# A two-layer transformer block on one core: both attentions rebuilt on row tiles and column strips, with key blocks brought in by DMA

## The chip, the core and the metric

The kernel runs on one core of one Trainium2 chip, as one program. A core has TensorE (matrix multiply), VectorE, ScalarE, GpSimd and SyncE, which here only issues DMAs. The engines run side by side and meet in semaphores. The metric is the time on the device in microseconds; the kernel before took 1709.56 us (median of three runs, 1708.59 to 1713.04).

## The reference, cut to what matters

`x` is 64 batches of 64 rows of 256 columns, `ctx` is 64 batches of 64 rows of 64 columns. There are four stages, each behind a layer norm and a gate.

```python
x = x + tanh(g_xattn[0]) * L0_xattn(layernorm(x), ctx, ctx)   # 32 heads of 8, 8 key heads
x = x + tanh(g_ffn[0])   * L0_ffn(layernorm(x), ...)          # 64 experts, top 8, and a shared one
x = x + tanh(g_xattn[1]) * L1_xattn(layernorm(x), ctx, ctx, Wc, bc)  # 16 heads of 16, 4 key heads, then @ Wc.T + bc
x = x + tanh(g_ffn[1])   * L1_ffn(layernorm(x), ...)          # two products on 8-bit grids
# an attention: the G = 4 query heads of a group share one key head
scores = einsum('bkgsd,bktd->bkgst', qh, kh) * d ** -0.5
out = einsum('bkgst,bktd->bkgsd', softmax(scores), vh)
```

## The kernel before, in words

The 4096 rows lie in SBUF as 32 tiles of 128 rows, two batches each. The program passes over all tiles once per stage, in this order: first attention, routing, experts (96 groups of four row blocks, fetched by SyncE from a DRAM table `xs`, results stored to `ys`), second attention, and the feed-forward. The second attention also adds the expert results into `x`: GpSimd issues 128 of the 256 indirect DMAs for that between its steps (`gather`, L632). While the first attention runs, SyncE loads the expert weights pair by pair (`pair`, L461 and L464, five DMAs), ScalarE rounds them to 16 bits into `region` (L729, L730), GpSimd takes the remainder (L606, L609), and SyncE also writes zeros into `xs` (`pads`, L479 and L481).

An attention is a software pipeline written out by hand for each engine: `step(t, j)` holds what that engine does in step `t` for tiles `t - 3` to `t + 3`, and `sweep` runs the steps from -3 to `LAST`. A tile needs: layer norm written to `XG` (L918, L919), a transpose to `Q1` (L1422, rounded to 16 bits at L738, remainder at L1028), products with the keys whose only use is the row maximum of each head (`maxima`, L1355, reduced at L982), a second transpose that brings remainder and maxima below the queries (`Q2`, L1435, L741), the scores (`scores`, L1369 and L1370), exponentials (L716), the products with the values (`values`, L1381), a copy, a transpose back (L1405), a division by the row sums and the sum into `x` (L1024). Different heads are kept apart by keys and values that are zero outside a head's own rows (`KD1`, `KD2`, `VD`); VectorE writes the key ones from a resident 16-bit copy of all keys, `KH` and its remainder `KL`, times a mask (`diagonal`, L971), and ScalarE the value ones (L757). Scores are products of 16-bit pairs over the whole array.

SyncE's loop in the first attention waits for GpSimd's remainder of pair `n - 2` before it loads pair `n` into the same buffer:

```python
for n in range(2, NPAIR):
    sp.wait_ge(wlo_done, 2 * (n - 1))
    if n > 2:
        sp.wait_ge(d_w, 80 * (n - 2))
    pair(n, stage[n % 2], d_w)
    pads(n - 2)
```

## Time and profile before

| what | value |
|---|---|
| time, median of three runs | 1709.56 us |
| profiled execution, its span | 1714.7 us (no other time is given for that execution) |
| first attention | to 296 us of the span |
| routing, then scatter and first half of the experts | 296 to 828 us |
| second half of the experts | 828 to 1156 us |
| second attention | 1156 to 1530 us |
| feed-forward | from 1530 us |
| busy share: TensorE, VectorE, ScalarE, GpSimd | 69%, 63%, 46%, 52% |
| DMA queue of SyncE | 234192 packets, 169.99 MB |

The shares are means over stages that are limited by different engines, so the rows further down are taken stage by stage. In the trace a row with SPq is SyncE at work on the issue of a DMA: its duration is what the issue costs SyncE, not how long the transfer takes. The boundaries of the stages are where the first and last instructions of their lines lie.

### The profile page before, as it was taken

To read this page: it belongs to the slowest core of one execution; us is meant where nothing else is said; L and a number is where in the kernel's file an instruction comes from. 1 tells how busy PE (TensorE), PEld (TensorE's weight loads), DVE (VectorE), ACT (ScalarE), POOL (GpSimd) and SP (SyncE) were. 2 spreads that over 40 slices of the span, in tenths; PEclk is the share of its full clock that TensorE was granted. 3 is DMA by queue.
4 is the path that set the end of the run, shared out by engine and by line. 5 is a ranking of instruction groups with operands and counts; after the bars stand their busy time and mean duration, and the time that the engine had idled before them with its cause. 6 is when DMAs were issued, how large, how long until landed. Compare 5 with 4: busy or idle time off the path is not lost.

```text
span 1714.7 us, 32329 instructions
## 1 busy us (share of the span) xinstructions
PE 1178.8 (69%) x9122; PEld 778.6 (45%) x9132; DVE 1084.7 (63%) x2699; ACT 783.1 (46%) x1599; POOL 883.5 (52%) x846
## 2 busy tenths in 40 slices
PE   4999998133333299999678777871676777846775
PEld 2566665112221266666555555650454444532243
DVE  5899996666666466666444454442765555747898
ACT  3566665122222166666445454441343333433574
POOL 2343343266666633333377777715888888516100
PEclk9999999555555599999777887785788888878878
DMA  9555554032323599999899999984344434100011
GB/s 209 161 151 154 148 154 135 15 115 104 111 106 110 154 281 308 310 301 304 206 242 237 252 246 248 247 199 101 53 54 55 55 55 55 28 1 1 13 37 49
DMA packets 283470, 247.09 MB, mean 144 GB/s; under 512 B 117584, under 2 KB 270032, under 8 KB 282960
## 3 DMA queue, kind: packets, MB, share of 16 engines
q1 hardware_dynamic: 234192, 169.99, 38.9%
q0 software_dynamic: 49152, 75.53, 20.8%
q8 instruction: 65, 1.06, 0.3%
q14 instruction: 61, 0.50, 0.1%
HBM read 111.93 MB, written 117.77 MB: 134 GB/s over the span
## 4 chain that ended last, share of the span: by engine, by line
DMA 24%; DVE 20%; PE 18%; POOL 16%; issue 13%; SPq 4%; ACT 3%; DVEq 1%; POOLq 0%; ACTq 0%
DMA xs<-V 13%; POOL x L632 11%; DMA arena<-xs 8%; PE bank L1493 4%; DVE arena L1318 3%; DMA xs<-arena,V 2%; PE bank L1369 2%; POOL rs L575 2%; PE bank L1381 2%; DVE arena L971 2%; PE bank L1355 2%; PE bank L1569 2%; PE bank L1370 2%; SPq L518 2%; DVE arena L1316 2%
## 5 line engine op out<-in xcount | busy, mean ns | idle before, releaser
L632 POOL DMA_INDIRECT x<-ys,idx x256 | 404.1, 1578 | 129.2 <-issue 57.6
L650 POOL DMA_INDIRECT xs<-V x192 | 187.1, 974 | 207.7 <-DMA xs<-V 188.5
L1493 PE MATMUL bank<-arena,region 128*128 128x128 f16 x2496 | 253.2, 245 | 1.6 <-ACT arena L834 0.9
L834 ACT COPY arena<-bank 128x640 f16<-128x640 f16 x192 | 132.3, 689 | 190.2 <-PE bank L1569 188.2
L1569 PE MATMUL bank<-arena 128*128 128x128 f16 x1440 | 145.2, 240 | 105.3 <-DMA arena<-xs 101.5
L1381 PE MATMUL bank<-arena 128*72 128x256 f32 (+1 forms) x768 | 212.0, 417 | 0.1
L1493 PEld LDWEIGHTS bank<-arena,region 128*128 (+1 forms) x2496 | 187.0, 111 | 19.2 <-issue 6.2
L1569 PEld LDWEIGHTS bank<-arena 128*128 128x128 f16 x1440 | 97.0, 107 | 113.3 <-DMA arena<-xs 85.4
L573 POOL TENSOR_TENSOR ve<-mv,epsilon 128x1 f32<-128x1 f32 x96 | 39.5, 412 | 202.0 <-DVE mv L912 180.0
L1381 PEld LDWEIGHTS bank<-arena 128*72 128x72 f32 (+1 forms) x768 | 117.2, 158 | 46.4 <-issue 13.5
L982 DVE TENSOR_REDUCE arena<-bank 128x8 f32<-128x512 f32 x192 | 124.1, 675 | 15.5 <-PE bank L1355 14.3
L1422 PE MATMUL bank<-cst,arena 128*128 128x128 f32 x256 | 50.5, 330 | 116.9 <-DVE arena L919 116.8
L716 ACT ACTIVATE arena<-bank 128x512 f32<-128x512 f32 x192 | 107.2, 593 | 27.2 <-PE bank L1370 24.3
L1598 PE MATMUL bank<-region,arena 128*128 x384 | 114.8, 299 | 6.4 <-DVE arena L1255 1.9
L1225 DVE COPY arena<-bank 128x640 f16<-128x640 f16 x96 | 46.7, 487 | 110.1 <-PE bank L1569 108.7
L1599 PE MATMUL bank<-region,arena 64*128 x384 | 113.5, 296 | 0.0
L1242 DVE TENSOR_TENSOR arena<-bank,arena 64x512 f32<-64x512 f32 x96 | 66.5, 693 | 73.0 <-ACT arena L847 73.0
L1624 PE MATMUL bank<-region 128*128 (+1 forms) x246 | 72.6, 430 | 47.1 <-ACT arena L892 17.8
L738 ACT CAST arena<-bank 128x512 f16<-128x512 f32 x64 | 37.4, 584 | 137.4 <-PE bank L1422 137.4
L919 DVE TENSOR_SCALAR arena<-x,mv,rs 128x256 f32<-128x256 f32 (+1 forms) x96 | 40.4, 421 | 92.6 <-POOL rs L575 92.4
L1369 PE MATMUL bank<-arena 128*128 128x256 f16 x384 | 96.6, 281 | 2.4 <-ACT arena L716 2.2
L1370 PE MATMUL bank<-arena 72*128 72x256 f16 (+1 forms) x384 | 95.8, 278 | 0.0
(204 smaller groups left out, 2557.6 us busy)
## 6 DMA issues: line engine op xcount, KB each, us to landing
ys<-arena SPq DMA_DIRECT2D x96, 512.0 KB
arena<-xs SPq DMA_DIRECT2D x288, 160.0 KB
xs<-idx SPq DMA_DIRECT2D x52, 256.0 KB, 2.4
arena<-in_wpairs SPq DMA_DIRECT2D x32, 256.0 KB, 2.6
arena<-in_wpairs SPq DMA_DIRECT2D x128, 64.0 KB, 2.5
x<-ys,idx POOLq DMA_INDIRECT x256, 6.3
out<-arena SPq DMA_DIRECT2D x16, 256.0 KB, 2.2
xs<-idx SPq DMA_DIRECT2D x52, 64.0 KB, 2.1
```

The lines of the kernel that those rows point to most:

```text
L632: pool.indirect_dma_start(tile_x(t), None, ys[t // HT], bass.IndirectOffsetOnAxis(ap=idx[:, t, k:k + 1], axis=0), compute_op=ALU.add).then ...
L650: pool.indirect_dma_start(xs[t // HT], bass.IndirectOffsetOnAxis(ap=at_row[:, t, n % 8:n % 8 + 1], axis=0), ROW[t % NROW], None).then_inc( ...
L716: act.activation(EX[(u + (0 if nsc == 2 else 2 * j)) % 4], bank[4 + u % 2][:, :], ACT.Exp, scale=d ** -0.5).then_inc(a["ex_ready"], 1)
L834: act.copy(XTP[g % 2][q], tpm[n % 2]).then_inc(R_["xt"], 1)
L982: dve.tensor_reduce(XG[j][:, u * gpu:(u + 1) * gpu, 2 * C:C + w], bank[2 + u % 2][:, :].rearrange("p (g k t) -> p g k t", g=gpu, t=S), AX. ...
L1369: pe.matmul(o, KD1[j][:, b, kc], Q1[j][:, :, b * S:(b + 1) * S], start=True, stop=False)
L1370: mm = pe.matmul(o, KD2[j][0:w, b, kc], Q2[j][0:w, :, b * S:(b + 1) * S], start=False, stop=True)
L1381: mm = pe.matmul(bank[6][0:w, b * 256:(b + 1) * 256], VD[j][:, b, p * w:(p + 1) * w], e[:, (p % 2) * 256:(p % 2 + 1) * 256], start=(p == 0 ...
L1493: mm = pe.matmul(o, lhs(a, w, k), rhs(a, w, k), start=(n == 0), stop=(n == 3 * KT - 1))
L1569: mm = pe.transpose(tpm[n % 2][:, m, :], RAW[g % 2][q][:, m * P:(m + 1) * P], rcv("ident"))
L1598: pe.matmul(o, IH[j][:, q, :], wx, start=True, stop=False)
L1599: mm = pe.matmul(o, IL[j][0:I, q, :], wx[0:I], start=False, stop=True)
```

## The change

Keys stay in float32 and are no longer rounded or masked. A ring of four buffers `KD` holds, for tile `t`, each key head on the partitions that its rows of the array have, and in the columns of its head, with zeros elsewhere. The zeros are written once per attention (VectorE before the first, GpSimd before the second), the rows of -1 that subtract the maximum once per buffer and pair of heads (`own_rows`: 16 DMAs of 2 partitions for the first attention, 8 for the second), and the keys themselves tile by tile by SyncE: one DMA per key head and tile (`keys`: eight DMAs of 8 partitions per tile in the first attention, four of 16 partitions in the second). The bulk loads of the transposed context, `KH`, `KL`, `KM` and the `diagonal` are gone.

TensorE's scores are one float32 product of 32 rows per pair of heads in the first attention (64 rows in the second) in place of two 16-bit ones over 128 and 72 rows; the maxima are products of 64 rows by 64 columns with 256 columns streamed (128 in the second); the values go to strips of 32 (64) output columns. Both transposes are of the full 128 by 128. VectorE writes 16-bit key blocks for the maxima from `KD` (`short_keys`, one or two operations on 256 elements), no longer computes a remainder of the queries, and writes the norm once. The value blocks of the first attention go from ScalarE to one GpSimd operation; GpSimd's remainders of the weights move one step later, and so do the values, the transposes back and all behind them: both sweeps are one step longer.

```diff
@@ sizes, tables
-LAST = (NT, NT + 2)
+LAST = (NT + 1, NT + 3)
+NKD = 4
...
-    KH = sb("KH", [P, B, S], F16)
-    KL = sb("KL", [P, B, S], F16)
+    KD = [sb(f"KD{n}", [P, 2, 2 * S]) for n in range(NKD)]
...
@@ SyncE
+            def own_rows(layer):
+                nk, d = LAYERS[layer]
+                a = CW + RCW + TCW + layer * 2 * S
+                rp = 2 * P // nk
+                for q in range(NKD):
+                    for n in range(nk // 2):
+                        at = slice(n * rp + 2 * d, n * rp + 2 * d + 2)
+                        sp.dma_start(KD[q][at], consts[at, a:a + 2 * S].unsqueeze(1).to_broadcast([2, 2, 2 * S])).then_inc(d_own, 16)
+
+            def keys(t, layer):
+                nk, d = LAYERS[layer]
+                if t >= NKD:
+                    sp.wait_ge(A[layer]["sc_ready"], (t - NKD + 1) * nk // 2)
+                for k in range(nk):
+                    at = k // 2 * (2 * P // nk) + k % 2 * d
+                    sp.dma_start(KD[t % NKD][at:at + d, :, k % 2 * S:(k % 2 + 1) * S],
+                                 ctxT[k * d:(k + 1) * d, 2 * t * S:2 * (t + 1) * S].rearrange("c (b s) -> c b s", b=2)).then_inc(d_kd[t % NKD], 16)
...
             for n in range(2, NPAIR):
+                if n + 2 < NT:
+                    keys(n + 2, 0)
                 sp.wait_ge(wlo_done, 2 * (n - 1))
...
+                if g == NG:
+                    sp.wait_ge(kd_zero, 2 * NKD)
+                    own_rows(1)
+                    for t in range(NKD):
+                        keys(t, 1)
...
+            for t in range(NKD, NT):
+                keys(t, 1)
@@ GpSimd, first attention
+                        pool.tensor_tensor(VD[1 - j].rearrange("p b (n h w) -> p (b n) h w", h=2, w=P // nk)[:, :, :, 0:d],
+                                           V[:, bass.ds((t + 1) * 2, 2), :].rearrange("p b (n h d) -> p (b n) h d", h=2, d=d),
+                                           ones[:, 0:2].unsqueeze(1).unsqueeze(3).to_broadcast([P, 2 * npair, 2, d]), ALU.mult).then_inc(a["vd_ready"], 1)
@@ VectorE
-                        diagonal(t + 2, KD1[j], KH, 0, a["kd_ready"])
-                        diagonal(t + 2, KD2[j], KL, 1, a["kl_ready"])
...
-                        dve.tensor_tensor(Q1[j][C:P], bank[0][C:P, :].rearrange("p (g s) -> p g s", g=G),
-                                          Q1[j][C:P], ALU.subtract).then_inc(a["q_ready"], 1)
...
+                def short_keys(t, q):
+                    if past(t, 2):
+                        dve.wait_ge(a["mx_ready"], (t - 1) * nmx)
+                    dve.wait_ge(d_kd[q], kd_done(t, q, layer))
+                    stand_alone(dve, side_v)
+                    for n in range(nk // 4):
+                        mm = dve.tensor_scalar(K16[q % 2][:, :, n * 2 * S:(n + 1) * 2 * S], KD[q][:, :, :], cv(f"part{layer}")[:, n:n + 1], None, ALU.mult)
+                    mm.then_inc(a["k16_ready"], 1)
@@ TensorE
-                            mm = pe.matmul(bank[2 + u % 2][b * S:(b + 1) * S, g * nk * S:(g + 1) * nk * S],
-                                           Q1[j][:, u * gpu + g, b * S:(b + 1) * S], KD1[j][:, b, 0:nk * S],
+                            for r in range(2):
+                                rows = slice(r * 64, (r + 1) * 64)
+                                last[r] = pe.matmul(bank[2 + r][b * S:(b + 1) * S, g * hk * S:(g + 1) * hk * S],
+                                                    Q1[j][rows, gp * 2 * gpu + g, b * S:(b + 1) * S], K16[j][rows, b, 0:hk * S],
+                                                    start=True, stop=True)
...
-                        pe.matmul(o, KD1[j][:, b, kc], Q1[j][:, :, b * S:(b + 1) * S], start=True, stop=False)
-                        mm = pe.matmul(o, KD2[j][0:w, b, kc], Q2[j][0:w, :, b * S:(b + 1) * S], start=False, stop=True)
+                            rows = slice(n * rp, (n + 1) * rp)
+                            mm = pe.matmul(bank[4 + n][:, b * 256:(b + 1) * 256], KD[q][rows, b, :], Q2[q % 2][rows, :, b * S:(b + 1) * S],
                                            start=True, stop=True)
...
-                        mm = pe.matmul(bank[6][0:w, b * 256:(b + 1) * 256], VD[j][:, b, p * w:(p + 1) * w],
-                                       e[:, (p % 2) * 256:(p % 2 + 1) * 256], start=(p == 0), stop=(p == npair - 1))
+                            mm = pe.matmul(bank[1][n * cg:(n + 1) * cg, b * 256:(b + 1) * 256], VD[j][:, b, n * cg:(n + 1) * cg],
+                                           EX[4 * j + n][:, b * 256:(b + 1) * 256], start=True, stop=True)
```

On SyncE the start of the program reads as follows, before and then after. `gate` is the small load of the gates, `V` the values, `x` the input, `in_wpairs` the weights.

```order
L446 DMA gate<-in_g_xattn 128x2
L446 DMA gate<-in_g_ffn 128x2
L451 DMA region<-in_ctxT 64x512 x2
L456 DMA V<-in_ctx 64x8x64 x2
L461 DMA arena<-in_wpairs 128x512
L464 DMA arena<-in_wpairs 64x256 x4
L461 DMA arena<-in_wpairs 128x512
L464 DMA arena<-in_wpairs 64x256 x4
L451 DMA region<-in_ctxT 64x3584 x2
L469 DMA x<-in_x 128x8x256
L456 DMA V<-in_ctx 64x56x64 x2
L471 DMA x<-in_x 128x20x256
```

```order
L445 DMA gate<-in_g_ffn 128x2
L454 DMA KD<-in_consts 2x2x128 x16
L462 DMA KD<-in_ctxT 8x2x64 x16
L468 DMA V<-in_ctx 64x8x64 x2
L476 DMA arena<-in_wpairs 128x512
L479 DMA arena<-in_wpairs 64x256 x4
L476 DMA arena<-in_wpairs 128x512
L479 DMA arena<-in_wpairs 64x256 x4
L462 DMA KD<-in_ctxT 8x2x64 x16
L485 DMA x<-in_x 128x8x256
L468 DMA V<-in_ctx 64x56x64 x2
L487 DMA x<-in_x 128x20x256
```

Four loads of the transposed context have become 48 small ones. In the loop over the pairs, one round on SyncE was and is:

```order
L461 DMA arena<-in_wpairs 128x512
L464 DMA arena<-in_wpairs 64x256 x4
L479 DMA xs<-idx 128x2x512
L479 DMA xs<-idx 128x2x128
L479 DMA xs<-idx 128x2x512
L479 DMA xs<-idx 128x2x128
```

```order
L462 DMA KD<-in_ctxT 8x2x64 x8
L476 DMA arena<-in_wpairs 128x512
L479 DMA arena<-in_wpairs 64x256 x4
L495 DMA xs<-idx 128x2x512
L495 DMA xs<-idx 128x2x128
L495 DMA xs<-idx 128x2x512
L495 DMA xs<-idx 128x2x128
```

The eight loads of keys stand ahead of the pair; rounds 2 to 29 have them, rounds 30 and 31 do not. In the second half of the experts SyncE had the first of these sequences between two groups and has the second, once:

```order
L518 DMA arena<-xs 128x640
L521 ISA
L521 DMA_TRANSPOSE arena<-xs 128x5x128
L527 DMA ys<-arena 128x4x256
L505 DMA V<-in_ctx 64x8x64 x2
```

```order
L539 ISA
L539 DMA_TRANSPOSE arena<-xs 128x5x128
L545 DMA ys<-arena 128x4x256
L454 DMA KD<-in_consts 2x2x128 x8
L462 DMA KD<-in_ctxT 16x2x64 x16
L523 DMA V<-in_ctx 64x8x64 x2
```

There 24 small loads stand between the store of one group and the fetch of a later one.

## Rows read from the trace of the kernel before

**Rows 1.** Windows by stage: busy us and instructions of each engine, granted clock, DMA.

```profile
core 0: us, PE busy (x) PEld busy (x) DVE busy (x) ACT busy (x) POOL busy (x), PEclk, DMA share, GB/s
39.00:296.00 257.00, 247.75 (x1580) 155.97 (x1580) 226.11 (x418) 161.00 (x336) 99.79 (x118) 0.99 0.53 153
828.00:1156.00 328.00, 256.76 (x2485) 189.62 (x2485) 147.01 (x294) 162.24 (x294) 200.28 (x128) 0.79 1.15 239
1156.00:1475.00 319.00, 199.81 (x1130) 133.65 (x1131) 180.68 (x429) 109.25 (x236) 263.09 (x261) 0.78 0.40 60
```

**Rows 2.** Waits of SyncE's queue, 100 to 200 us.

```profile
SPq L461 <- POOL region L609: 35.9, 12, 3.1
```

**Rows 3.** Timeline of SyncE, one row step (start, duration).

```profile
250.20 0.35 SPq L461 DMA_DIRECT2D arena<-in_wpairs  x1
250.60 2.40 SPq L464 DMA_DIRECT2D arena<-in_wpairs  x4
253.04 2.18 SPq L479 DMA_DIRECT2D xs<-idx  x4
258.36 0.35 SPq L461 DMA_DIRECT2D arena<-in_wpairs  x1
```

**Rows 4.** Timeline of SyncE, start of the program.

```profile
2.15 0.51 SPq L446 DMA_DIRECT2D gate<-in_g_xattn  x1
4.43 1.33 SPq L456 DMA_DIRECT2D V<-in_ctx  x2
11.98 1.23 SPq L451 DMA_DIRECT2D region<-in_ctxT  x2
13.88 15.35 SPq L456 DMA_DIRECT2D V<-in_ctx  x2
29.28 5.65 SPq L471 DMA_DIRECT2D x<-in_x  x1
39.02 1.60 SPq L461 DMA_DIRECT2D arena<-in_wpairs  x1
```

**Rows 5.** Issues of three lines: minimum, median, maximum in ns.

```profile
L464 SPq DMA_DIRECT2D arena<-in_wpairs x48: 471/596/599, 103.9 to 195.3; - x48
L451 SPq DMA_DIRECT2D region<-in_ctxT x4: 582/592/596, 3.2 to 12.6; - x4
L518 SPq DMA_DIRECT2D arena<-xs x144: 332/338/2487, 829.5 to 1133.6; - x144
```

**Rows 6.** Groups by line and form, 100 to 260 us.

```profile
L918 DVE TENSOR_SCALAR arena<-x,mv,rs 128x256 f32 x20 | 23.1, 1157 | 1.2
L1028 DVE TENSOR_TENSOR arena<-bank,arena 64x512 f16<-64x512 f32 x20 | 13.9, 695 | 0.6
L971 DVE TENSOR_TENSOR arena<-KL,arena 128x1024 f16<-128x1024 f16 x19 | 13.0, 682 | 0.0
```

**Rows 7.** Timeline of TensorE, 150 to 156 us.

```profile
149.95 0.62 PE L1355 MATMUL bank<-arena 128*64 128x512 f16 x4 [0.16 <-DVE arena L1028]
153.90 1.89 PE L1381 MATMUL bank<-arena 128*72 128x256 f32 x8
155.62 0.60 PE L1435 MATMUL bank<-cst,arena 128*72 128x128 f32 x4
```

**Rows 8.** Timeline of SyncE, second half of the experts.

```profile
841.86 2.34 SPq L518 DMA_DIRECT2D arena<-xs  x3
...
845.66 0.52 SPq L527 DMA_DIRECT2D ys<-arena  x1
846.22 1.87 SPq L505 DMA_DIRECT2D V<-in_ctx  x2
```

**Rows 9.** Groups by line, second attention, 1200 to 1450 us.

```profile
L632 POOL DMA_INDIRECT x<-ys,idx x104 | 166.1, 1598 | 28.7 <-issue 28.7
```

**Rows 10.** Timeline of VectorE, end of the second attention.

```profile
1488.28 0.68 DVE L982 TENSOR_REDUCE arena<-bank 128x8 f32<-128x512 f32 x1
1494.96 0.68 DVE L982 TENSOR_REDUCE arena<-bank 128x8 f32<-128x512 f32 x1
```

More of the change, by code:

```diff
@@ L136, in tile_table, with own_table @@
     return t
-def mask_table():
+def own_table():
     r, out = np.arange(P)[:, None], []
     for nk, d in LAYERS:
-        k = np.arange(nk)[None, :]
-        own = (r % C) // d == k
-        signed = np.where(r < C, r // d == k, -1.0 * (r - C == k))
-        out += [np.repeat(m.astype(np.float16), S, axis=1) for m in (own, signed)]
-    return np.ascontiguousarray(np.concatenate(out, axis=1)).view(np.float32)
+        out.append(np.repeat(-1.0 * (r % (2 * P // nk) - 2 * d == np.arange(2)[None, :]), S, axis=1))
+    return np.concatenate(out, axis=1).astype(np.float32)
 def const_table():
-    return np.concatenate([attention_table(), route_table(), tile_table(), mask_table()], axis=1)
+    return np.concatenate([attention_table(), route_table(), tile_table(), own_table()], axis=1)
 def known(t):
@@ L456, in values @@
                     sp.dma_start(V[half * S:(half + 1) * S, b0:b1, :], ctx[b0:b1].rearrange("b t c -> t b c")).then_inc(d_ctx[part], 16)
-            keys(0)
+            sp.wait_ge(kd_zero, NKD)
+            own_rows(0)
+            for t in range(2):
+                keys(t, 0)
             values(0)
@@ L467, in _ @@
                 pair(n, stage[n], d_stage[n])
-            keys(1)
+            for t in range(2, NKD):
+                keys(t, 0)
             sp.dma_start(x[:, 4:12, :], xv[:, 4:12, :]).then_inc(d_x[1], 16)
@@ L587, in attention @@
                     pool.memset(VD[j].rearrange("p b w -> p (b w)"), 0.0).then_inc(a["vd_set"], 1)
+                for q in range(NKD):
+                    pool.memset(XG[q].rearrange("p g w -> p (g w)"), 0.0).then_inc(a["vd_set"], 1)
                 pool.wait_ge(a["vd_set"], 2)
@@ L619, in attention @@
                             gather(HT, n)
-                        step(t, t % 2)
+                        step(t, t % NKD)
                         if t == -2:
@@ L637, in _ @@
             pool.wait_ge(A[0]["x_done"], NT)
+            for q in range(NKD):
+                pool.memset(KD[q][:, :, :].rearrange("p b t -> p (b t)"), 0.0).then_inc(kd_zero, 1)
             for t in range(0, NT, LNB):
@@ L1386, in step, with maxima @@
-                def step(t, j):
-                    if inside(t + 1):
-                        pe.wait_ge(a["q_ready"], t + 2)
-                        pe.wait_ge(a["kd_ready"], t + 2)
-                        for u in range(nmx // 2):
-                            maxima(t + 1, 1 - j, u)
+                def maxima(t, j, gp):
+                    if past(t, 1) or gp >= 1:
+                        pe.wait_ge(a["mx_done"], t * nmx + 2 * gp)
+                    stand_alone(pe, side_p)
+                    last = [None, None]
+                    for g in range(2 * gpu):
+                        for b in range(2):
+                            for r in range(2):
[3 more added lines that the diff above has]
+                                                    start=True, stop=True)
+                    for mm in last:
+                        mm.then_inc(a["mx_ready"], 1)
@@ new lines, in scores @@
+                def scores(t, q):
+                    if past(t, 1):
+                        pe.wait_ge(a["ex_ready"], t * npair)
+                    rp = P // npair
+                    for b in range(2):
+                        for n in range(npair):
+                            rows = slice(n * rp, (n + 1) * rp)
+                            mm = pe.matmul(bank[4 + n][:, b * 256:(b + 1) * 256], KD[q][rows, b, :], Q2[q % 2][rows, :, b * S:(b + 1) * S],
+                                           start=True, stop=True)
+                            if b:
+                                mm.then_inc(a["sc_ready"], 1)
@@ L1392, in step @@
+                def step(t, q):
+                    j = q % 2
+                    if inside(t - 2):
+                        pe.wait_ge(a["pvs_ready"], t - 1)
+                        for g in range(G):
+                            mm = pe.transpose(bank[1][:, g * P:(g + 1) * P], PVS[:, g, :], ident)
+                        mm.then_inc(a["ot_ready"], 1)
                     if inside(t):
                         pe.wait_ge(a["q2_ready"], t + 1)
-                        pe.wait_ge(a["kl_ready"], t + 1)
@@ L1408, in step @@
-                    if inside(t):
-                        for u in range(nsc, 2 * nsc):
-                            scores(t, j, u)
+                        scores(t, q)
                     if inside(t + 1):
-                        for u in range(nmx // 2, nmx):
-                            maxima(t + 1, 1 - j, u)
+                        for gp in range(1, nmx // 2):
+                            maxima(t + 1, 1 - j, gp)
                     if inside(t + 2):
```

447 lines of the change are left out of this document (201 added, 246 removed).

## The prediction, on record before the changed kernel ran

> **What bounds the kernel now.** I read the stages first. In the first attention [rows 1] the reader should see TensorE busy for 247.75 of 257 us and VectorE for 226.11: both are nearly full, ScalarE and GpSimd are not, and the clock is granted at 0.99. In the second attention GpSimd is busy for 263.09 of 319 us and no other engine comes near. The steps of the first attention repeat every 8.14 to 8.16 us, read from the starts of one SyncE line in two rounds, 250.20 and 258.36 [rows 3].
>
> The engine that the page does not list is the one I looked at longest, since the change gives it most. SyncE works on each DMA that it issues for 0.35 to 0.60 us. One round in the first attention is 0.35 + 2.40 + 2.18 and gaps, from 250.20 to 255.22: 5.02 us for nine DMAs [rows 3]. Then it waits for GpSimd, 35.9 us in 12 rounds, 3.0 us each [rows 2]; from the rows, 258.36 - 255.22 = 3.14 us. That is all the room there is.
>
> **The first attention, compute.** TensorE. Before, a stream of 256 columns in 16 bits takes 256/2.4 = 107 ns if it is alone, one of 512 columns 213 ns, and a float32 product of 256 columns 0.43 us, since four of them (eight instructions) start at 153.90 and the next line at 155.62 [rows 7]. After: 8 scores and 8 values in float32, 16 maxima of 256 columns and 12 transposes at some 0.13 us (the four at 155.62 take 0.60 us with the last one's way out). End to end that is 3.4 + 3.4 + 1.7 + 1.5 = 10.0 us, more than now. Four row tiles or four strips side by side make it 0.9 + 0.9 + 0.4 + 1.5 = 3.7 us. The trace has something of the kind: four maxima of 512 columns in two column halves take 0.62 us in all, where four alone would need 4 x 0.213 = 0.85 [rows 7]. So halves do overlap, and I count on strips and row tiles overlapping too. The Trainium skill says so as well (TensorE: Matmul & The Clock Gate, Part 3: packing small matmuls): matmuls in different row groups or column groups run concurrently, and four row tiles gained 3.07 times there. No run here has shown row tiles yet.
>
> VectorE works 226.11/257 x 8.14 = 7.2 us per step. The remainder of the queries (0.69), both diagonals (0.68 each as listed, which overlap a little, 1.2 together) and the second write of the norm (1157 ns, of which some 0.4 is the operation and the rest waiting beside GpSimd) go [rows 6]; two operations on 256 elements, 0.4 us each, come. That leaves 7.2 - 0.7 - 1.2 - 0.8 + 0.8 = 5.3, up to 6.6 if each of the three tensor-scalar operations waits beside GpSimd as long as the first norm write does now. ScalarE is busy 161.00/257 x 8.14 = 5.1 us and loses the value blocks. The engines that compute could therefore do a step in about 6.5 us.
>
> **The first attention, SyncE.** Each round gets eight more issues, and they must fit into 3.14 us: 0.39 us each. What an issue of 8 partitions and two runs of 64 elements costs no row shows. From below: the fetch of expert rows, 0.338 us at the median [rows 5], some 0.38 with the gap to the next. From above: 1.33 us for two loads of values, 0.67 each [rows 4]. The nearest rows: loads to 64 partitions cost 0.592 to 0.596 us in two different lines, however many bytes they carry [rows 5], and the gates, the smallest load, 0.51 us [rows 4], some 0.55 with the gap. The new loads are narrow and small; I take 0.55 us from start to start. A round is then 5.02 + 8 x 0.55 = 9.4 us, and SyncE no longer waits: TensorE and VectorE wait for it, through the keys (needed two tiles ahead by VectorE) and through the weights (ScalarE copies pair t at the end of its step t). With 0.38 it is 8.1, no step shorter than now; with 0.67 it is 10.4.
>
> Start of the program: 48 such issues instead of four. Up to the gates SyncE needs 2.7 us (one DMA less). From 4.43 to the end of the last load of x at 34.93 there are 30.5 us, less 1.27 for the two context loads at 11.98, so 29.2 us that stay (the long one, 15.35, is a queue that is full, and stays by my estimate) [rows 4]. Round 2 then starts at 2.7 + 29.2 + 48 x 0.55 = 58.3 us, where now it starts at 39.02. 28 rounds with keys at 9.42 us and 2 us for the larger first one end at 324; two without keys, 11 us, at 335; from there the last pair has to land, be split, and the pipeline has to empty, one step more than now, 9 us: 344 us. Now it ends at 296. So +48 us for the stage. The same sum with 0.38: 50 + 230 + 20 = 300, +4 us; with 0.67: 64 + 293 + 20 = 377, +81 us.
>
> The Trainium skill has a sentence that speaks against this whole term (DMA: Bandwidth & Descriptors, Issuing engines are not separate DMA queues): the sequencer's time to initiate a DMA "is usually small relative to the DMA itself". By it the first attention would fall to the step of the compute engines, the rival below. The trace agrees only in part: a weight load takes 0.60 us to issue and 2.4 to land, but the issues are serial and fill 5.02 of 8.14 us.
>
> **The stages behind it.** Routing and scatter wait for the first attention and shift with it, nothing in them is touched; four zero fills on GpSimd lie beside VectorE's statistics: 0. Second half of the experts: SyncE is busy from 841.86 to 848.1 almost without a gap [rows 8], and now issues 24 small loads in one go, 13.2 us at 0.55. The fetches run three groups ahead, about 13 us at the 4.4 us between groups there, but of that the landing of the next fetch has to be paid; the stage also moves data for all its time (DMA share 1.15) [rows 1]. I charge half, +7 us, bounds 0 and +16 (24 x 0.67).
>
> Second attention: the 104 gathers of 250 us take 166.1 us and 28.7 us of issue gaps, and with the small operations GpSimd never pauses [rows 9]. The change leaves that work as it is, so a lighter VectorE and TensorE gain nothing until the gathers end at 1475. Four key DMAs per step, 2.2 us, are hidden in a step of over 10 us. Behind the gathers VectorE sets the step: 1494.96 - 1488.28 = 6.68 us [rows 10]. It loses the remainder, two diagonals and a norm write and gets one operation, about 1 us, in some six full steps; the sweep has one step more at 4 us, so -6 + 4 = -2, and I write -3 us with the first load of the masks gone; bounds -8 and +5.
>
> Sum: 48 + 7 - 3 = +52 us. The span is 1714.7 us, 5.1 above the median of the runs. On the span that makes 1766.7 and on the median 1709.56 + 52 = 1761.6 us.
>
> **The rivals.** A: small loads are cheap to issue, 0.2 us or less. Then SyncE's round is 6.6 us and the compute engines set 6.6 us as well: 42 us of start, 30 steps of 6.6 and 10 of tail make 250 us, -46; experts +2, second attention -3: 1709.6 - 47 = 1663 us. For it: the bytes are few (4 KB). Against it: the gates carry 1 KB and cost as much as any; no issue in the trace is under 0.33 us. By the skill's sentence this would be the outcome. B, no change: issues of 0.36 to 0.40 us, SyncE at 8.1 us or just under, the sum within 5 us of now: 1713 us. C: the strips and row tiles do not overlap in float32. Then TensorE needs 10.0 us per step and with waits 10.3: (10.3 - 8.14) x 30 = +65, start +10, experts +4, and the second attention, where float32 scores come on top, 0: 1789 us, whatever SyncE costs. Against it stands the overlap of the halves in 16 bits [rows 7]. A slower clock adds nothing by itself: at half of it TensorE's 3.7 us are 7.4, still under 9.4.
>
> **How the numbers follow.** 5 us, 0.3%, is about what a measurement can tell from no change. The forecast, SyncE bound with 0.40 to 0.67 us per issue, has 0.66; its own range is 1718 (4 + 4 + 0) to 1800 (81 + 12 - 3). C has 0.08. A has 0.20, of which about half lies at 0.30 us per issue, round 7.4, nearer to 1690. B has 0.06. Slower 0.74, same 0.06, faster 0.20. The predicted time is 1761 us. The range of 8 in 10 leaves out half of A below and the far end of C and of the forecast above: 1680 to 1800.
>
> **What would show it.** SyncE in the first attention without a wait longer than 0.3 us, rounds 9.4 us apart, key issues near 0.5 us, and VectorE waiting for the landing of keys or ScalarE for weights; the granted clock well under 0.99, since TensorE idles; the first attention ending near 344 us; one gap in the experts of some 7 us behind the 24 loads; GpSimd's gathers back to back as now in the second attention. Wrong is the whole forecast if SyncE still waits for GpSimd in each round, or if a key issue takes 0.3 us or less; C shows as rows of four products one after the other.

## The result and the profile after

| | changed | before, same chip | ratio |
|---|---|---|---|
| median | 1720.4 us (1714.2 to 1725.4, 20 runs) | 1709.5 us (1704.7 to 1717.8, 20 runs) | 1.0056, 95% interval 1.0043 to 1.0070 |
| span of the profiled execution | 1720.5 us | 1714.7 us | |

Slower, as forecast, but by about 10 us and not by 52. The trace places the 5.8 us between the two spans by four landmarks: the start of the last update of the first attention 295.8 → 292.8 (-3.0), which is what "the first attention ends at" means from here on; from there to the last store of expert rows 857.6 → 862.4 (+4.8); from there to the last update of the second attention 377.1 → 380.5 (+3.4); and the rest +0.6. The spans are of one execution each, and the one before was longer than its median by 5 us, so they differ by less than the medians do.

The same windows as in [rows 1], columns as there:

```profile
39.00:296.00 257.00, 165.82 (x1757) 94.98 (x1756) 142.12 (x346) 140.79 (x267) 103.97 (x149) 0.82 0.56 162
828.00:1156.00 328.00, 251.94 (x2466) 185.72 (x2464) 148.31 (x294) 161.08 (x293) 199.05 (x128) 0.80 1.16 233
1156.00:1475.00 319.00, 184.27 (x1324) 122.76 (x1324) 148.62 (x341) 106.20 (x231) 263.86 (x264) 0.76 0.42 64
```

In the first attention TensorE was busy for 82 us less and VectorE for 84 us less, and the stage is only 3 us shorter. The waits of 100 to 200 us (us in total, times, the longest), first SyncE's queue, to be read against [rows 2], then the engines:

```profile
SPq L476 <- POOL region L624: 0.2, 1, 0.2
...
POOL ve L595 <- DVE mv L1036: 33.1, 12, 3.9
PE bank L1413 <- DVE arena L1000: 30.6, 12, 4.0
DVE arena L1013 <- DMA KD<-in_ctxT: 30.0, 12, 3.6
```

SyncE's 35.9 us of waiting have become 0.2. VectorE now waits in each step for the keys to land, and TensorE and GpSimd for VectorE. One round on SyncE, as in [rows 3]:

```profile
149.89 0.36 SPq L476 DMA_DIRECT2D arena<-in_wpairs  x1
150.29 2.39 SPq L479 DMA_DIRECT2D arena<-in_wpairs  x4
152.72 2.16 SPq L495 DMA_DIRECT2D xs<-idx  x4
154.93 2.80 SPq L462 DMA_DIRECT2D KD<-in_ctxT  x8
157.83 0.36 SPq L476 DMA_DIRECT2D arena<-in_wpairs  x1
```

There is no pause in it: 5.0 us for the old nine DMAs, 2.8 for eight key loads, 7.94 us from pair to pair. This is a quick round. Over the 28 rounds from 48.69 to 277.96 the mean is 8.19 us, where it was 8.41. Over the 22 rounds behind the first five (from 92.74 to 271.71, before from 87.30 to 266.50) it is 8.14, where it was 8.15; these 22 rounds are called the steady ones below. So the steady round is what it was. The -3 comes from the ends of the stage: its third pair starts 9.7 us later, 4.2 us of that are back after five rounds, 1.6 in all the rest, and 6.9 are won behind the start of the last pair (9.3 us from there to the last update, 16.2 before). What an issue costs (ns, minimum, median, maximum), as in [rows 5]:

```profile
L462 SPq DMA_DIRECT2D KD<-in_ctxT x184: 273/299/1524, 64.4 to 247.5; - x184
L454 SPq DMA_DIRECT2D KD<-in_consts x24: 237/258/694, 2.7 to 842.2; - x24
L479 SPq DMA_DIRECT2D arena<-in_wpairs x88: 471/596/778, 59.8 to 233.3; - x88
```

The start of the program, against [rows 4]:

```profile
2.70 4.82 SPq L454 DMA_DIRECT2D KD<-in_consts  x16
7.56 5.39 SPq L462 DMA_DIRECT2D KD<-in_ctxT  x16
...
20.63 5.62 SPq L462 DMA_DIRECT2D KD<-in_ctxT  x16
26.29 0.40 SPq L485 DMA_DIRECT2D x<-in_x  x1
26.73 7.72 SPq L468 DMA_DIRECT2D V<-in_ctx  x2
34.50 5.70 SPq L487 DMA_DIRECT2D x<-in_x  x1
40.32 8.32 SPq L462 DMA_DIRECT2D KD<-in_ctxT  x8
```

### The profile page after: what moved, and what is told of

Read it like the earlier page. It is cut to its first block, busy times and chain, and to the rows that moved or that the text cites. A ratio compares the mean times of both kernels' runs of the same rounds, so it can differ in the third digit from the quotient of the medians.

```text
span 1720.5 us, 33063 instructions
## 1 busy us (share of the span) xinstructions
PE 1080.4 (63%) x9644; PEld 707.6 (41%) x9644; DVE 964.9 (56%) x2538; ACT 760.4 (44%) x1530; POOL 888.7 (52%) x889
## 4 chain that ended last, share of the span: by engine, by line
DMA 23%; SPq 16%; issue 16%; POOL 16%; DVE 14%; PE 11%; ACT 3%; DVEq 0%; POOLq 0%; ACTq 0%
DMA xs<-V 14%; POOL x L672 11%; DMA arena<-xs 7%; SPq L462 4%; SPq L479 3%; PE bank L1507 3%; SPq L495 3%; DVE arena L1345 3%; POOL rs L597 2%; PE bank L1583 2%; SPq L536 2%; DVE arena L1343 2%; SPq L523 1%; POOL x L632 1%; DVE HM L1318 1%
## 5 line engine op out<-in xcount | busy, mean ns | idle before, releaser
L1413 PE MATMUL bank<-arena 128*32 128x256 f32 (+1 forms) x768 | 90.1, 471 | 135.7 <-DVE arena L1000 132.1
L928 DVE TENSOR_SCALAR arena<-x,mv,rs 128x256 f32<-128x256 f32 (+1 forms) x96 | 53.5, 558 | 177.2 <-POOL rs L597 177.2
L595 POOL TENSOR_TENSOR ve<-mv,epsilon 128x1 f32<-128x1 f32 x96 | 33.5, 349 | 149.0 <-DVE mv L1036 95.6
L1413 PEld LDWEIGHTS bank<-arena 128*32 128x32 f32 (+1 forms) x768 | 39.3, 138 | 162.8 <-issue 158.2
L759 ACT COPY arena<-bank 128x512 f32<-128x512 f32 x64 | 37.7, 589 | 143.3 <-PE bank L1413 143.3
L868 ACT CAST arena<-arena 64x512 f16<-64x512 f32 x96 | 59.3, 618 | 72.9 <-DVE arena L1269 52.4
L692 POOL DMA_INDIRECT xs<-arena,V x64 | 64.2, 1002 | 48.6 <-DMA xs<-arena,V 27.2
```

What stands on the lines that cost most here:

```text
L692: pool.indirect_dma_start(xs[t // HT], bass.IndirectOffsetOnAxis(ap=at_row[:, t, n % 8:n % 8 + 1], axis=0), ROW[t % NROW], None).then_inc( ...
L1413: mm = pe.matmul(bank[1][n * cg:(n + 1) * cg, b * 256:(b + 1) * 256], VD[j][:, b, n * cg:(n + 1) * cg], EX[4 * j + n][:, b * 256:(b + 1) * ...
```

## The experiments

In the experiments on the first attention T1 is the theory that its round is the sum of what SyncE needs to issue its DMAs; in the last two it is what their expectation says. Ratios are to the kernel before, run on the same chip in the same job.

### Is it the issues? Key loads left out, weight loads merged, the same merges in the kernel before

```diff
@@ e1_no_keys: tiles 4 to 31 compute on the keys of tiles 0 to 3
-                if n + 2 < NT:
-                    keys(n + 2, 0)
@@ e2_weights: both experts of a half in one DMA, 3 loads per pair instead of 5
-                for e in range(2):
-                    for half in range(2):
-                        sp.dma_start(dst[1][half * I:(half + 1) * I, e, :], ...)
+                for half in range(2):
+                    sp.dma_start(dst[1][half * I:(half + 1) * I, :, :], wpairs[...].rearrange("(e i) a w -> i e (a w)", e=2))
@@ e3_both and e4_before_both: also the zero fills
-                pads(n - 2)
+                if n % 2:
+                    pads((n - 3) // 2)      # twice as many experts per fill
```

> The changed kernel without the key loads of tiles 4 to 31 in the first attention (each ring buffer keeps its first tile's keys, so the scores are computed on other keys; all compute instructions stay). SyncE's round falls from about 8.2 us (0.36 + 2.4 + 2.2 + 2.8 and gaps) to 5.0. Theory T1 (the rate of SyncE's issues sets the step of the first attention): the step falls to what the compute engines need, 6.5 us at a guess from VectorE's 5.3 busy us, 28 rounds x 1.7 = 47 us less than the changed kernel, about 1673, and SyncE waits for GpSimd again. Rival T2 (the step is set by the chain through TensorE at its lower clock and the landing of transfers): step stays at 8 us, time within 5 us of the changed kernel, 1715 to 1725.

Measured: 1640.8 us, ratio 0.959 (0.956 to 0.962). The first attention ends at 215.0, 78 us earlier than in the changed kernel. SyncE's timeline:

```profile
151.71 0.44 SPq L478 DMA_DIRECT2D arena<-in_wpairs  x1
152.19 2.39 SPq L481 DMA_DIRECT2D arena<-in_wpairs  x4
154.62 2.16 SPq L497 DMA_DIRECT2D xs<-idx  x4
156.88 0.44 SPq L478 DMA_DIRECT2D arena<-in_wpairs  x1
```

The quick round is 5.17 us, and between 100 and 200 us SyncE waits for nobody. So T1 holds, more strongly than I expected: SyncE was to wait for GpSimd again and does not, since the compute engines can do a step in 5.2 us or less, not in the 6.5 to 6.6 that I had put as their limit. The mean of the steady rounds is 5.34 us here and 8.14 in the changed kernel: 2.8 us for eight key loads, 0.35 each. The quick rounds say the same (7.94 - 5.17).

> The changed kernel, same work and same bytes, with the four loads of the second weight (64 x 256 each) made two loads of 64 x 2 x 256. T1: two issues of 0.6 us fewer per round, so the round falls by about 1.2 us in each of the 30 rounds and the program by 28 to 36 us, to about 1688. T2: no change, 1715 to 1725.

Measured: 1692.1 us, ratio 0.987 (0.984 to 0.990); the first attention ends at 269.3. Two issues less save 24 us over the stage and 28 us in the medians, where T1 said 28 to 36: T1 holds, a little short. The steady round goes from 8.1 to 7.3 us.

> The kernel BEFORE with the same two merges. There SyncE waits 3 us in each round, so fewer issues can only lengthen that wait: no change, within 5 us of 1709.5, by both theories. If it gains 10 us or more, the merges help by something other than SyncE's issue rate (the DMA queues), and runs 2 and 3 prove less.

Measured: 1710.3 us, ratio 1.0003 (0.998 to 1.002). Where SyncE has 3 us to spare in a round [rows 2], fewer issues are worth nothing in the total; the stage itself ends 3 us earlier, at 292.7.

> As the run before, and the zero fills of the expert table issued every second round at double size (2.2 us of issue per two rounds in place of 4.4). T1: SyncE's round is then 5.8 us on average, below the compute step of some 6.5, so it goes as far as the run without key loads: about 1673 to 1680, and SyncE waits again. T2: no change.

Measured: 1705.7 us, ratio 0.997 (0.995 to 0.999), the first attention ends at 281.6: a miss. Still fewer issues than in the run with merged weights alone made it 12 us slower in that stage. Here SyncE waits for GpSimd again, 11.7 us in 7 rounds between 100 and 200 us, so the plain sum of issues no longer sets the pace. This is taken up below.

### What does an issue cost by? One load for two tiles

```diff
+            def keys2(t):
+                    sp.wait_ge(A[0]["sc_ready"], (t - NKD + 2) * nk // 2)
+                for k in range(nk):
+                    sp.dma_start(KDA[at:at + d, q:q + 2, :, ...], ctxT[k * d:(k + 1) * d, 2 * t * S:2 * (t + 2) * S]...)
...
-                if n + 2 < NT:
-                    keys(n + 2, 0)
+                if n % 2 == 0 and n + 2 < NT:
+                    keys2(n + 2)
```

> The changed kernel, but in the first attention one load brings a block of key rows for two tiles (8 partitions by 4 runs of 64 numbers) instead of one tile, in every second round: 8 issues in two rounds instead of 16, the same bytes; and 4 loads of constant rows instead of 16 at its start. T1 (an issue costs mostly by itself, by the 16-partition loads of as many runs 0.42 us): two rounds hold 5.0 x 2 + 8 x 0.42 = 13.5 us of issues instead of 16.4; the round without keys meets what stopped the kernel with doubled zero fills near 6.2 us, so a pair of rounds takes 14.6, 14.5 pairs save 26 us, the start 5: the first attention ends near 262, time about 1690 us, ratio 0.988. T2 (an issue costs by the runs that it moves): a double load costs 0.70, rounds stay at 8.1 us, only the start gains: 1714 to 1717 us. T3 (keys that come later, since the double load must wait for the scores of one tile more, stall VectorE): slower than the changed kernel.

Measured: 1687.2 us, ratio 0.984 (0.981 to 0.988), the first attention ends at 262.4 (T1: 262). SyncE's timeline, a round with keys and one without:

```profile
160.25 2.81 SPq L479 DMA_DIRECT2D KDA<-in_ctxT  x8
163.16 0.36 SPq L492 DMA_DIRECT2D arena<-in_wpairs  x1
163.56 2.39 SPq L495 DMA_DIRECT2D arena<-in_wpairs  x4
165.99 2.18 SPq L510 DMA_DIRECT2D xs<-idx  x4
169.59 0.36 SPq L492 DMA_DIRECT2D arena<-in_wpairs  x1
```

Eight loads of twice the bytes and twice the runs take 2.81 us, the same as the single ones (2.80); the merged weight loads show the same (0.63 us for 128 KB, 0.60 for 64). In these shapes the price is per DMA, and T2 is excluded. In the round without keys SyncE has a pause again (168.17 to 169.59; 8.0 us in 100). The Trainium skill (DMA: Bandwidth & Descriptors, Rules for kernel authors) advises to coalesce many small transfers, since under 64 KB one pays mostly overhead. This run agrees for the issue: loads of 4 KB and of 8 KB cost SyncE the same.

### Number or order? Where the key loads stand in the queue

The order alone, in the changed kernel:

```diff
-                if n + 2 < NT:
-                    keys(n + 2, 0)
                 ...
                 pair(n, stage[n % 2], d_w)
+                if n + 3 < NT:
+                    keys(n + 3, 0)
                 pads(n - 2)
```

> The changed kernel with the same 16 issues in a round of the first attention, in another order: the weights of a pair first, then the keys of the tile one further on, then the zero fills, so that the keys no longer stand behind the fills of the round before. T1 (the sum of SyncE's issues is the round): 2.8 + 2.8 + 2.2 us and the gaps are the same, the round stays at 8.1 us, first attention ends within 3 us of 293, 1717 to 1722 us. T2 (the round is a loop through the keys' landing behind the fills, as with the doubled fills, where the order alone made 1696 or 1646 us): rounds of 6 to 7 us, the first attention 30 us or more shorter, 1690 us or less. T3 (the keys wait for scores that come too late, and the fills and the next weights wait behind them): slower than 1722 us.

Measured: 1718.9 us, ratio 1.0030 (1.0014 to 1.0046), the first attention ends at 289.9. T1: VectorE still waits 28.7 us for keys in 100, SyncE does not pause, the order is worth at most the 3 us. The keys come late because SyncE is late.

Then where SyncE has time. The base is the version with loads for two tiles in both attentions, merged weights, the small loads of the second attention spread, and a later reduction:

> The loads for two tiles in both attentions (in the second one 10 small loads instead of 24, one per group of the experts), two weight loads less per pair of experts, and GpSimd's reduction one step later, all in the changed kernel. T1 (SyncE's issues bound the first attention): a round with keys issues 3.4 + 1.7 + 2.2 = 7.3 us, one without 3.9, where compute takes 5.2 to 6.2; the mean round is 6.3 to 6.8 us instead of 8.1, first attention 40 to 52 us shorter, start 6, experts 9, tail 4: 1650 to 1665 us, ratio 0.965 to 0.974. T2 (with the issues gone the keys' landing or TensorE's clock bounds the round at 7.3 or more): 1680 us or more.

Measured: 1663.9 us, ratio 0.971 (0.968 to 0.974), in time as T1. The first attention ends at 244.9; a pair of rounds takes 13.9 us, a little more than T1's 12.6 to 13.6, because only the round with keys is full of issues: in the others SyncE waits for GpSimd, 17.1 us in 100, and VectorE for keys, 15.2 us. On it stand two versions with the same 18 DMAs in each pair of rounds, which differ in the round that holds the doubled zero fills:

```diff
@@ e10_fills_odd: order is pair, fills, keys, pair
+                if n % 2:
+                    pads((n - 3) // 2)
@@ e11_fills_even: order is keys, pair, fills, pair
+                if n % 2 == 0:
+                    pads((n - 2) // 2)
```

> The version with loads for two tiles in both attentions, two weight loads less and the later reduction (1664 us, ratio 0.971; a round with keys took 7.1 us, one without 5.9 to 6.8), now with the zero fills of two rounds in one, of double size, in the rounds without keys, just ahead of the next key loads. T1 (only the number of SyncE's issues counts): 4.7 us of issues in a round with keys, 4.8 in one without, so both go at the 5.2 us of the kernel without key loads: the first attention 35 us shorter, about 1625 to 1635 us. T2 (what slowed the changed kernel with doubled fills, 281.6 against 269.3 us at the end of its first attention, is that key loads behind a doubled fill are held up in the queues, in issue and in landing): no gain or a loss, 1660 to 1680 us.

> As the kernel before it in this group, but the doubled fills stand in the rounds with keys, behind the key and weight loads, a whole round away from the next keys. T1 (only issues count): a round with keys has 2.8 + 1.7 + 3.0 = 7.5 us of issues, one without 1.7: mean of 7.5 and 5.2 to 6.2, 6.4 to 6.9, 1655 to 1664 us, worse than with the fills in the other rounds. T2 (keys behind doubled fills are held up): the same 6.4 to 6.9, but better than the other order or equal to it.

Measured: 1695.8 us (ratio 0.991, 0.988 to 0.994) with the fills ahead of the keys, 1646.3 us (0.962, 0.957 to 0.966) with the fills behind keys and weights. T1 is excluded and T2 holds, with a size beyond my numbers both ways: 50 us between two orders of the same issues. The first attention ends at 275.3 and 224.4. The fills ahead of the keys, timeline of SyncE and of VectorE's first use of the keys:

```profile
160.12 0.36 SPq L487 DMA_DIRECT2D arena<-in_wpairs  x1
160.52 1.25 SPq L489 DMA_DIRECT2D arena<-in_wpairs  x2
161.83 3.50 SPq L504 DMA_DIRECT2D xs<-idx  x4
165.37 4.75 SPq L474 DMA_DIRECT2D KDA<-in_ctxT  x8
...
155.15 0.61 DVE L1023 TENSOR_SCALAR arena<-KDA,cst 128x256 f16<-128x256 f32 x2 [2.96 <-DMA KDA<-in_ctxT]
171.37 0.61 DVE L1023 TENSOR_SCALAR arena<-KDA,cst 128x256 f16<-128x256 f32 x2 [4.43 <-DMA KDA<-in_ctxT]
```

VectorE has keys at 155.15; SyncE stands until 160.12, first for the landing of the weights that it has just issued (14.1 us in 6 places of 100 us), then for GpSimd's remainder (14.9 us in 6), which the compute behind those keys releases; pair, fills and keys then take until 170.12, and at 171.37 VectorE has the next keys. That is a loop of 5.0 + 11.25 = 16.2 us for two rounds, with SyncE idle in one part of it (155.63 to 160.12) and VectorE for the last 4.43 us of the other. The key loads behind doubled fills cost 4.75 us instead of 2.8; that full queues are the reason is my reading, no row shows a queue. In these rows the hold-up is in the issue and not in the landing: VectorE has the keys 1.25 us after SyncE is done with them (170.12 to 171.37), and with the other order 1.45. The fills behind keys and weights:

```profile
156.93 2.90 SPq L474 DMA_DIRECT2D KDA<-in_ctxT  x8
159.93 0.36 SPq L487 DMA_DIRECT2D arena<-in_wpairs  x1
160.33 1.26 SPq L489 DMA_DIRECT2D arena<-in_wpairs  x2
161.62 2.98 SPq L504 DMA_DIRECT2D xs<-idx  x4
167.42 0.36 SPq L487 DMA_DIRECT2D arena<-in_wpairs  x1
```

Keys take 2.9 us, and SyncE's pause (164.60 to 167.42) lies behind everything that somebody waits for. This is also how I read the miss above, where the order alone was not tried: there too the doubled fills stood right ahead of the keys of the next round (2.88 us of fills, 4.14 of keys).

### More buffers, and the fills halved

```diff
@@ e12_ring, on the version of 1663.9 us
+RING = 8
...
+                if n + 4 - n % 2 < NT:
+                    keys2(n + 4 - n % 2, 0, range(4 * (n % 2), 4 * (n % 2) + 4))
@@ e14_ring_fills, on e12_ring: doubled fills of one half of the rows per round
-                pads(n - 2)
+                pads((n - 2) // 2, n % 2)
```

> The version of 1664 us with key buffers for 8 tiles instead of 4: the 8 loads of two tiles are split, 4 in each round, and go out one to two rounds earlier; the zero fills as in the changed kernel. T1 (in that version a round with keys is bound by 7.1 us of issues and the next by keys that land late, VectorE waits 15.2 us for them in 100 us): every round has 1.4 + 1.7 + 2.2 = 5.3 us of issues with their gaps 5.5, keys are never waited for, the round goes to 5.5 to 5.8 us instead of 6.9: the first attention 30 to 40 us shorter, 1625 to 1635 us, ratio 0.949 to 0.955. T2 (compute of one step takes 6.2 us or more once keys are there, and the 5.2 us without key loads came from less traffic): 1640 to 1650 us.

Measured: 1639.8 us, ratio 0.958 (0.955 to 0.960). Three rounds from 150.22 to 167.54 take 5.77 us each, the mean of the steady ones is 5.91, VectorE waits for no keys, and the first attention ends at 220.6, 24 us earlier than in the version it is built on, where 30 to 40 were expected. It is T1 in kind: SyncE waits only 3.5 us in 100. In the total it lies 5 us above T1's range and at the edge of T2's.

> The version with key buffers for 8 tiles (1640 us, ratio 0.958, rounds of 5.75 us, SyncE without a pause), and the zero fills of one half of the rows in each round at double size: 2 fill issues in a round instead of 4, every round alike. T1 (its round is still the sum of issues): 1.6 us of fills instead of 2.26, the round goes to 5.1 to 5.3 us, 28 rounds save 12 to 17 us: 1623 to 1630 us, ratio 0.948 to 0.952. T2 (the round is bound by the weights' landing and the engines by now, ScalarE waited 23.4 us in 100 for the weights): 1636 to 1644 us.

Measured: 1633.9 us, ratio 0.951 (0.948 to 0.955), the best version of all. Its round:

```profile
150.39 0.36 SPq L488 DMA_DIRECT2D arena<-in_wpairs  x1
150.79 1.25 SPq L490 DMA_DIRECT2D arena<-in_wpairs  x2
152.09 1.15 SPq L505 DMA_DIRECT2D xs<-idx  x2
153.28 2.33 SPq L475 DMA_DIRECT2D KDA<-in_ctxT  x4
155.71 0.36 SPq L488 DMA_DIRECT2D arena<-in_wpairs  x1
```

5.3 us without a pause (the mean of the steady rounds is 5.53, and SyncE waits 6.7 us in 100), of which the four key loads now take 2.33 us, where they took 1.6 to 1.8 in the version before it (median 0.43 each against 0.31): part of what the fills gave back the loads took, with the DMA engines at 0.75 of their time. The stage is 9 us shorter; between T1 and T2 in the total.

### The two small terms

```diff
@@ e5_spread: one of the 24 small loads per group of the experts, instead of all at once
+                if NG <= g < NG + 24:
+                    small_load(g - NG)
@@ e6_tail
-                        if t == NT - 1:
+                        if t == NT:
                             pool.partition_all_reduce(FS[:, 14:15], FS[:, 1:2], P, RMAX)
```

In the changed kernel the 24 loads and the pause behind them read as follows on SyncE and VectorE, against [rows 8]:

```profile
839.45 3.00 SPq L454 DMA_DIRECT2D KD<-in_consts  x8
842.49 7.32 SPq L462 DMA_DIRECT2D KD<-in_ctxT  x16
849.85 1.38 SPq L523 DMA_DIRECT2D V<-in_ctx  x2
...
861.03 0.49 DVE L1252 COPY arena<-bank 128x640 f16<-128x640 f16 x1 [14.07 <-issue]
```

> The changed kernel, but the 24 small loads for the second attention (8 of constant rows, 16 of keys) go out one per group of the experts' second half instead of all in one go. T1 (SyncE's block of 13.2 us of issues holds back a token fetch, and VectorE waits for it: its line of rescued inputs waited 25.6 us in 7 places, 14.1 at most): the second half of the experts loses the stall, the last store of expert rows comes 8 to 10 us earlier than in the changed kernel, about 1711 us, ratio 1.001 to the kernel before. T2 (the groups absorb the stall later, or the 9.9 us come from the clock or from the gathered keys' landing): the last store within 2 us, 1719 to 1721 us.

Measured: 1713.9 us, ratio 1.0002 (0.998 to 1.002). From the end of the first attention to the last store it takes 855.0 us, against 862.4 in the changed kernel and 857.6 before. T1. One pair of traces alone would be weak, since this stretch moves by some us from trace to trace. Over all versions it is 857.6 to 863.5 us with the 24 loads in one go (seven traces, mean 861), 851.4 to 860.0 with small loads spread over the groups (six, mean 854.5), and 857.6 and 851.1 in the kernel before, as it is and with merged loads. So the stall was worth about 7 us, and all of the stage's loss is gone with it.

> The changed kernel, but GpSimd's reduction over all partitions stands one step later in the second attention, behind the statistics of one tile more, as many steps from the end as in the kernel before. T1 (after the reduction three tiles' statistics are left instead of two, and VectorE waits 10.9 us there for GpSimd): the last update comes 4 to 5 us earlier, 1715 to 1716 us, ratio 1.003 to 1.004. T2 (the end of the attention is bound by the chain through TensorE, with the reduction hidden beside it, or the result of the reduction is needed so late now that the last stage pays what the steps win): 1720 us.

Measured: 1722.6 us, ratio 1.0052 (1.0028 to 1.0076): T2. The last update comes 380.1 us behind the last store, where it was 380.5; the reduction itself starts later instead (1524.2, in the changed kernel 1522.3, though the gathers ended 2.3 us earlier). The place of the reduction is not what the added step costs.

## Why the prediction was right in its mechanism and wrong in its size

**The direction: partly luck.** "Slower" rested on +48 us in the first attention. That stage came out 3 us shorter, and the kernel is slower by the two small terms, of which one was forecast with the other sign.

**SyncE becomes the bound: right.** It said that SyncE would issue without a wait longer than 0.3 us, that VectorE would wait for keys, and that the granted clock would fall well under 0.99. Between 100 and 200 us the trace has one wait of 0.2 us and 30.0 us of VectorE waiting for keys, and the clock was 0.82 from 39 to 296 us. Leaving the key loads out gives 80 us back; the same merges help here and do nothing in the kernel before.

**The price of a key issue: the step that failed.** "The new loads are narrow and small; I take 0.55 us from start to start." It is 0.299 us at the median and 0.35 from start to start, the same by the run without them. In the forecast's own sum (5.02 + 8 x price) a steady round of 8.14 us means 0.39, since the old nine DMAs have slower moments too. That is the lower bound of the range I had written down, 0.38 from the fetch row of 0.338 [rows 5], and the sum at that bound was already there: a round of 8.1 us, the stage +4. Measured are 8.1 us and -3. One of my own signs of being wrong, "a key issue takes 0.3 us or less", is met at the median; it was badly chosen, since eight such issues with their gaps still fill the room of 3.14 us. I went by the nearest rows in width, 0.59 to 0.60 for 64 partitions and 0.51 for the gates, as if they bounded a narrow load from below. They do not: the rows of this kernel now read 0.258 us for 2 partitions, 0.299 for 8, 0.423 for 16 at the median (the second attention's loads), 0.596 for 64. The rows [rows 5] alone did not show that, but they did show that the price does not grow with the width: 128 partitions at 0.338 against 64 at 0.592. A price that goes both ways with the shape has no nearest row. The middle of the bounds, 0.52, would have missed too: what the rows allowed was the whole interval, with more than 0.06 for its lower end.

**The start of the program: mis-sized in two terms.** Forecast was round 2 at 58.3 us; it begins at 40.32. The 48 loads take 15.8 us instead of 26.4. The long load of values was "a queue that is full, and stays"; it went from 15.35 to 7.72 us [rows 4]. It did not shrink because SyncE had spent more time ahead of it: in the version of 1663.9 us it is issued about as early as before and is as short,

```profile
15.39 7.55 SPq L480 DMA_DIRECT2D V<-in_ctx  x2
```

and in the kernel before with merged loads, issued at 11.61, it takes 15.71 us. What the long ones have ahead of them and the short ones have not are the two bulk loads of the transposed context, 1.8 MB, which the change removed. The forecast took off the 1.27 us of their issue and not what they made the next load wait. Some of it came back in round 2, whose keys take 8.32 us instead of 2.8.

**The sum.** The stage's end was off by 51 us (344 forecast, 293 measured): 18 by the start; 28 by the 28 rounds with keys (237.6 us from 40.32 to 277.96, forecast 265.8); nothing by the two rounds without keys (11.4 us, forecast 11); and 5 behind them (4 us instead of 9), a third term that was too large. The forecast's own range, 1718 to 1800 us, was not added up from its terms' bounds (0 and 16 for the experts, -8 and +5 for the second attention); with them it is 1706 to 1812.

**Experts: +7 forecast, +4.8 measured**, about 7 over all traces, and the run with spread loads gives 7.4 back. The mechanism stands: the loads take 10.3 us (forecast 13.2), and VectorE has one gap of 14.07 us behind them, where that line waits 4.8 us at most for TensorE elsewhere in the stage. The gap is twice the 7 us forecast for it; part of it is made up later.

**Second attention: -3 forecast, +3.4 measured.** GpSimd's last gather starts at 1475.0 where it started at 1475.1, as said; the loss lies behind it, 5.3 us to the last update. Two terms failed there. In the changed kernel, and the last updates of both:

```profile
1481.93 1.28 DVE L988 TENSOR_REDUCE arena<-bank 128x8 f32<-128x512 f32 x2
1488.16 1.28 DVE L988 TENSOR_REDUCE arena<-bank 128x8 f32<-128x512 f32 x2
...
1535.68 0.48 DVE L1075 SCALAR_TENSOR_TENSOR x<-bank,tg,x 128x256 f32<-128x256 f32 x1 [0.78 <-PE bank L1462]
```

```profile
1530.55 0.47 DVE L1046 SCALAR_TENSOR_TENSOR x<-bank,tg,x 128x256 f32<-128x256 f32 x1
```

A full step is 6.24 us where it was 6.68 [rows 10], 0.4 less and not 1 less; the first of them takes 8.25 us, so that the five steps up to the last row maxima gain nothing (33.2 us, before 33.0). From there to the last update it takes 28.8 us instead of 23.25: the added step costs 5.5, not the 4 that I had charged. Moving the reduction changed nothing. Why it is 5.5 was not tried.

**The rivals.** A (cheap issues, 1663 us) supposed 0.2 us, and half of its chance lay at 0.30; no key load took under 0.273, and 0.30 at the median gave a round of 8.1 us and not the 7.4 that A had for it, which left out the gaps and the slower moments. Its second part, compute steps of 6.6 us, was wrong as well: with SyncE out of the way they take 5.2 or less. C, no overlap in float32, is excluded: in the version with eight key buffers, at a granted clock of 0.98, TensorE shows

```profile
153.24 1.15 PE L1411 MATMUL bank<-arena,KDA 32*128 32x256 f32 x16
154.31 0.41 PE L1397 MATMUL bank<-arena 64*64 64x256 f16 x8
155.46 1.07 PE L1425 MATMUL bank<-arena 128*32 128x256 f32 x16
```

Eight float32 products (16 instructions) take 1.15 us on row tiles and 1.07 on strips, where one after the other at 0.43 us [rows 7] they would take 3.4: three times faster. That agrees with the 3.07 that the Trainium skill gives for four row tiles (TensorE: Matmul & The Clock Gate, Part 3: Packing small matmuls), here in float32, with 256 columns, and for strips too. B, no change at issues of 0.36 to 0.40 us and 1713 us, had about the right price, and for the first attention the right outcome; the two small terms made the rest. It was given 0.06.

**The sentence of the Trainium skill** that the time to initiate a DMA "is usually small relative to the DMA itself" (DMA: Bandwidth & Descriptors, Issuing engines are not separate DMA queues) holds for one load only in part (a weight load takes 0.60 us to issue and 2.4 to land; no row gives the landing of a key load) and does not help with the loop: issues alone fill the round in the changed kernel and in the one without keys, and all but 7% of it in the best version. The weighing in the prediction was right.

## What to carry to other kernels

Count the DMAs of a loop against the time that the issuing engine has left in it: here eight small loads took all of the 3.1 us of room, and what the change saved on the other engines, some 3 us per step by the run without key loads, lay behind that. Merge loads until the loop is bound by something else (two tiles per load, two experts per load: the price is per DMA), then put what is waited for ahead of what is not: where the issuing engine had pauses, the same issues in another order were 50 us apart, and where it had none, the order was worth 3 us at most. Where no row shows the price of a new shape, and the known prices do not run one way with size, forecast from the whole interval, not from the row that looks alike.

## What the runs showed of the hardware that I had not expected

- The price of an issue on SyncE by shape: 0.258 us (2 partitions), 0.299 (8, two or four runs of 64 numbers alike), 0.423 (16), 0.596 (64), 0.338 (128, expert rows). For 8 partitions it rose with what stood ahead: 0.43 at the median with the DMA engines 0.75 busy, 0.59 on average right behind doubled fills.
- An issue that looks expensive can be paying for what was queued ahead of it: the long load of values took 15.35 and 15.71 us behind 1.8 MB of context loads (issued at 13.88 and 11.61 us) and 7.5 to 7.9 us without them (issued between 15.39 and 26.74).
- The granted clock of the first attention, between 40 and 200 us, was 0.98 before, 0.81 in the changed kernel, 0.91 at rounds of 6.95 us and 0.98 again in the two versions with eight key buffers. TensorE was busy for 155, 103, 116, 127 and 134 of the 160 us. Where SyncE issued without a pause the clock did not set the round. Where SyncE waited for compute, as with the doubled fills ahead of the keys (0.86 from 100 to 200 us), a part of that wait may be the slower clock; it was not tried.
